# Moving the layer norm, the last group's context parts and the route scatters to other steps of an attention and expert kernel

## The reference

```
s = attention(xn)            # 16 heads of 32, causal, a bias per head that grows with distance
g = silu(ffn(xn))            # router picks one of 2 experts per token:
                             #   h = xn @ w_fc[e].T ; a = where(h >= 0, h, h / 2) ** 2
                             #   out = (a @ w_proj[e].T) * probability of the chosen expert
x = x + s * g
```

## Time and profile before

| | |
|---|---|
| median of 3 runs | 1466.62 us |
| the profiled execution | 1466.41 us |
| its span in the trace | 1464.6 us |
| TensorE busy | 1367.3 us, 93% |
| VectorE, ScalarE, GpSimd busy | 930.0, 773.3, 692.3 us |
| iteration -1 (to the first transposed head) | 66.86 us |
| batches 0 to 7, in order | 81.1, 85.5, 85.6, 85.5, 87.2, 85.5, 85.5, 80.7 us |
| last projections and the experts' part | 721.0 us |

### The profile page before, as it was taken

How to read it: one execution, slowest core, us unless ns; L and a number is a source line. 1 busy time by engine, 2 the same in 40 slices (tenths; PEclk the granted TensorE clock), 3 DMA queues, 4 the chain that set the end, 5 groups by cost and what they waited for, 6 DMA issues and landing times.

```text
span 1464.6 us, 30064 instructions
## 1 busy us (share of the span) xinstructions
PE 1367.3 (93%) x9755; PEld 868.8 (59%) x9755; DVE 930.0 (64%) x2441; ACT 773.3 (53%) x1824; POOL 692.3 (47%) x896
## 2 busy tenths in 40 slices
PE   2879999999999999999779999999999999999995
PEld 1455555655556565555546666666666666666663
DVE  7577777777767777777759955554445555544443
ACT  3478778787878778777846522222222222223221
POOL 0356657465665747566624443433343433333332
PEclk9999999999999999999999999999999999999998
DMA  4435334343533434335347422211111122111100
GB/s 162 145 87 148 125 114 128 107 140 109 148 120 121 126 102 139 112 119 146 103 142 232 148 56 58 53 38 43 55 55 53 50 58 58 43 38 51 46 30 30
DMA packets 119458, 140.56 MB, mean 96 GB/s; under 512 B 48655, under 2 KB 97807, under 8 KB 117136
## 3 DMA queue, kind: packets, MB, share of 16 engines
q1 hardware_dynamic: 110368, 112.81, 25.6%
q0 software_dynamic: 8944, 25.83, 5.7%
HBM read 97.81 MB, written 33.95 MB: 90 GB/s over the span
## 4 chain that ended last, share of the span: by engine, by line
PE 78%; DVE 8%; POOL 6%; ACT 3%; issue 2%; DMA 1%; SPq 0%; DVEq 0%; POOLq 0%; ACTq 0%
PE psF L1142 22%; PE psY L1162 22%; PE psA L353 18%; PE psT L447 7%; PE psA L462 5%; POOL pr L942 4%; PE psS L426 3%; POOL route L970 1%; PE psA L410 1%; DVE pr L858 1%; DVE stat L750 1%; DVE am L637 1%; DVE xT L764 1%; DVE wf L1269 1%; POOL rstd L957 1%
## 5 line engine op out<-in xcount | busy, mean ns | idle before, releaser
L1142 PE MATMUL psF<-xT,wf 128*128 128x256 f16 (+1 forms) x3264 | 368.0, 269 | 0.0
L1162 PE MATMUL psY<-wf,aT 128*128 x1584 | 363.9, 379 | 0.5 <-DVE aT L1322 0.4
L1142 PEld LDWEIGHTS psF<-xT,wf 128*128 x3264 | 312.0, 98 | 63.5
L942 POOL TENSOR_SCALAR pr<-pr,rden 128x128 f32<-128x128 f32 (+3 forms) x512 | 269.9, 546 | 139.9 <-DVE rden L869 138.4
L1396 POOL TENSOR_TENSOR a<-a 128x512 f32<-128x512 f32 (+1 forms) x136 | 156.0, 1147 | 370.4 <-DVE a L1313 369.9
L580 ACT ACTIVATE pr<-pr,mn 128x128 f32<-128x128 f32 (+3 forms) x512 | 282.1, 554 | 0.0
L858 DVE CUSTOM_DVE_ANT_0 pr<-psS,base,nsl 128x128 f32<-128x128 f32 (+3 forms) x512 | 249.7, 543 | 4.0 <-PE psS L426 4.0
L1162 PEld LDWEIGHTS psY<-wf,aT 128*128 128x128 f16 x1584 | 154.5, 98 | 159.0 <-issue 1.4
L447 PE MATMUL psT<-conf,pr 128*128 128x128 f32 x1280 | 205.6, 279 | 18.5 <-POOL pr L942 16.7
L447 PEld LDWEIGHTS psT<-conf,pr 128*128 128x128 f32 x1280 | 156.9, 142 | 81.8 <-POOL pr L942 27.9
L353 PE MATMUL psA<-xT,wqkv 128*128 128x512 f16 x768 | 188.4, 385 | 14.8 <-DVE wqkv L668 13.1
(11 more groups left out here) (157 smaller groups left out, 1352.3 us busy)
## 6 DMA issues: line engine op xcount, KB each, us to landing
qk_parts<-pre SPq DMA_DIRECT2D x64, 256.0 KB, 2.7
qs<-qk_parts SPq DMA_DIRECT2D x128, 128.0 KB, 2.7
ks<-qk_parts SPq DMA_DIRECT2D x128, 128.0 KB, 2.7
wst<-in_wf SPq DMA_DIRECT2D x16, 1024.0 KB
wstage<-in_wf SPq DMA_DIRECT2D x32, 512.0 KB, 4.8
xin<-in_x SPq DMA_DIRECT2D x32, 256.0 KB, 4.5
attn_out<-so SPq DMA_DIRECT2D x32, 256.0 KB, 2.0
xT<-wstage SPq DMA_TRANSPOSE x216, 2.4
```

Source lines behind the costliest of these rows:

```text
L942: nc.gpsimd.tensor_scalar(p_, p_, rden[:, c:c + 1], 32768.0, ALU.mult, ALU.mult).then_inc(s["norm_done"], 1)
L1142: last = nc.tensor.matmul(psF[c % 2][:, k * TT:k * TT + tn], w(e, 2 * hc, hl, kc * 512 + col, P), xT[:, r % 2, x, kc, 0:tn], start=(m == 0 ...
L1162: last = nc.tensor.matmul(psY[r % 2][h][:], aT[:, c % 4, x, k, h * P:(h + 1) * P], w(e, 2 * hc + 1, hl, q * 512, 512), start=(c == 0 and k ...
```

## The change

VectorE: statistics move ahead of the step's casts, within steps 0 and 1. The cast of the last group's context moves from step 2 to step 1, between `masked` and the statistics. Rows are made in steps 3 to 6. GpSimd: the deviations move from step 1 to step 2, ahead of the step's low part. The low part of the last group's context moves from step 2 to step 1, ahead of the low part of k. The scatters of a batch are issued in the next iteration, one in each of steps 4 to 7 (for the last batch two in each of steps 4 and 5).

```diff
+            def context_high(pb, pg):
+                if within(pb, 0, B):
+                    wait(dve, s["ctx_staged"], pb * NG + pg + 1)
+                    wait(dve, s["O_done"], pb * QB + 1)
+                    nc.vector.tensor_copy(cx[:, pg, 0, :], cf[:]).then_inc(s["ctx_hi"], 1)
+
@@ att_vector, iteration
                 masked(3)
+                if step == 1:
+                    context_high(b - 1, NG - 1)
+                if more and step < 2:
+                    ln_stats(2 * step)
+                    ln_stats(2 * step + 1)
                 for args in jobs(b, odd, step, ("q", "k", "x", "o", "logits", "rank")):
                     read_out(*args)
                 turned(2)
-                if more:
-                    if step < 2:
-                        ln_stats(2 * step)
-                        ln_stats(2 * step + 1)
-                    elif step < 6:
-                        ln_apply(step - 2)
+                if more and 3 <= step < 7:
+                    ln_apply(step - 3)
...
-                if j == (3 if g else 2):
-
-                    pb, pg = (b, g - 1) if g else (b - 1, NG - 1)
-                    if within(pb, 0, B):
-                        wait(dve, s["ctx_staged"], pb * NG + pg + 1)
-                        wait(dve, s["O_done"], pb * QB + 1)
-                        nc.vector.tensor_copy(cx[:, pg, 0, :], cf[:]).then_inc(s["ctx_hi"], 1)
+                if g and j == 3:
+                    context_high(b, g - 1)
@@ att_gpsimd
+        def context_low(pb, pg):
+            if within(pb, 0, B):
+                wait(pool, s["ctx_hi"], pb * NG + pg + 1)
+                nc.gpsimd.tensor_tensor(cx[:, pg, 1, :], cf[:], cx[:, pg, 0, :], ALU.subtract
+                                        ).then_inc(s["ctx_lo"], 1)
+
@@ att_gpsimd, iteration (after the norms)
-                for kind, bj, i, _, _ in jobs(b, odd, step, ("q", "k")):
-...
-                if more and step == 1:
+                if more and step == 2:
 ...
-                pb, pg = (b, g - 1) if g else (b - 1, NG - 1)
-                if j == (3 if g else 2) and within(pb, 0, B):
-...
+                if step == 1:
+                    context_low(b - 1, NG - 1)
+                for kind, bj, i, _, _ in jobs(b, odd, step, ("q", "k")):
+...
+                if g and j == 3:
+                    context_low(b, g - 1)
                 if b == B - 1 and step in (10, 12):
                     ffn["gather_x"](pool, 0, 0, (step // 2 - 5,))
-                if more and step in (14, 15):
-
-                    wait(pool, s["meta_ready"], nxt + 1, s["apart_pool"])
-                    for i in (2 * step - 28, 2 * step - 27):
+                if within(b, 0, B) and 4 <= step < (6 if b == B - 1 else 8):
+                    pool.wait_ge(s["meta_ready"], b + 1)
+                    for i in ((2 * step - 8, 2 * step - 7) if b == B - 1 else (step - 4,)):
                         nc.gpsimd.indirect_dma_start(
```

More of the change, by code:

```diff
@@ L958, in iteration @@
                                             ).then_inc(s["rstd_ready"], 1)
-                pb, pg = (b, g - 1) if g else (b - 1, NG - 1)
-                if j == (3 if g else 2) and within(pb, 0, B):
-                    wait(pool, s["ctx_hi"], pb * NG + pg + 1, s["apart_pool"])
-                    nc.gpsimd.tensor_tensor(cx[:, pg, 1, :], cf[:], cx[:, pg, 0, :], ALU.subtract
-                                            ).then_inc(s["ctx_lo"], 1)
+                if step == 1:
+                    context_low(b - 1, NG - 1)
+                for kind, bj, i, _, _ in jobs(b, odd, step, ("q", "k")):
+                    w = int(kind == "k")
+                    wait(pool, s["qk_hi"], (bj * NG + i) * 2 + 1 + w, s["apart_pool"])
+                    nc.gpsimd.tensor_tensor(pre[:, w, 1, :], stage[:, w, :], pre[:, w, 0, :],
+                                            ALU.subtract).then_inc(s["qk_lo"], 1)
+                if g and j == 3:
+                    context_low(b, g - 1)
                 if b == B - 1 and step in (10, 12):
                     ffn["gather_x"](pool, 0, 0, (step // 2 - 5,))
-                if more and step in (14, 15):
-                    wait(pool, s["meta_ready"], nxt + 1, s["apart_pool"])
-                    for i in (2 * step - 28, 2 * step - 27):
+                if within(b, 0, B) and 4 <= step < (6 if b == B - 1 else 8):
+                    pool.wait_ge(s["meta_ready"], b + 1)
+                    for i in ((2 * step - 8, 2 * step - 7) if b == B - 1 else (step - 4,)):
                         nc.gpsimd.indirect_dma_start(
```

## The result

The changed kernel takes 1442.28 us, the median of four runs (1440.97 to 1443.58); the kernel before takes 1467.02 us beside it on the same chip (four runs, 1462.87 to 1468.66). The ratio is 0.9836, with a 95% interval of 0.9813 to 0.9858. The prediction was 1447.5 in a range of 1442 to 1456: right in sign and in mechanism, with the time only 0.3 above the low end. The profiled execution took 1442.62 us with a span of 1440.8, so the span is 23.8 us shorter, where the sum said 18.9.

A forecast was written before the change was run, and what follows sets the result against it. TensorE was taken as the bound, its transposes waiting 16.7 us for GpSimd's norms. Terms 15.2 + 2.0 + 1.4 + 2.1 - 1.2 - 1.1 + 0.5 = 18.9 us gave 1447.5, range 1442 to 1456.

The forecast's parts named there:

- the sum: Whole execution: gains and losses of all terms add to 18.9 us, from 1466.4 to 1447.5.
- Statistics, deviations, context: Steps 0 to 3: earlier norms of head 3 (2.06 us) remove step 3's 2.68 us wait; 2.54 gained per full batch.
- 0.14, as predicted: Step 4 of a full batch: TensorE still waits 0.14 us for the norms of head 4.
- The turn of the batch: Between batches: the 0.21 us wait goes, with its restart worth 0.3 us, seven times, 2.1 us.
- Block 2's row: Step 6, batches 1 to 6: the row comes too late for its transposes, costing 0.2 us six times, 1.2 us.
- The wait predicted at 0.74: Start of step 6: TensorE waits 0.74 us for block 2's row; 0.40 left by idle time, 0.13 by starts.
- Batch 0: Gains 2.0 us, from its 1.77 wait and a short wait of the scores; pays nothing for block 2's row.
- Iterations -1 and 8: Iteration -1: last block copy and weight scales later, -1.1 us; iteration 8: context's cast leaves earlier, +0.5 us.
- The clock: Batch 4, after step 3's wait: the granted clock may no longer fall, up to 1.6 us more gain.
- The queue does not stay late: Rival, GpSimd's steps 1 to 3: norms still take 2.72 us, 0.65 less gain in seven batches, 1452 to 1456; 17%.
- the wait does not move a step on: Rival: all of the 2.5 us comes back before step 4, about 1464.5, no change; 7%.
- Scatters do not get in front of norms: Rival, steps 6 and 7, spare 2.6 and 2.2 us: scatters of 5 us each would give 1482, slower; 4%.

The follow-up runs named there:

- 2: Kernel before, with only the statistics moved ahead of the casts of steps 0 and 1: 1458.12 us, periods of 84.84.
- 3: Changed kernel, with both parts of the last group's context put back at the end of step 2: 1454.81 us, periods of 84.03.
- 4: Changed kernel, with deviations back in step 1 behind the low part of k and rows back in steps 2 to 5: 1450.45 us.
- 10: Changed kernel, with the deviations' instruction given twice: 1450.9 us, periods of 83.87.
- 11: Changed kernel, with the deviations' instruction given three times: 1461.84 us, periods of 85.20.
- experiment 1: Kernel before, with only the scatters moved to steps 4 to 7: 1466.03 us, periods of 85.06.
- experiment 5: Changed kernel, with step 6's projection put ahead of block 2's transposes: 1445.55 us, periods of 82.57.
- experiment 8: Changed kernel, with projection first in step 6, first weight reduction in step 4 instead of 5, iteration -1's rows in steps 2 to 5: 1436.83 us.
- experiment 6: Changed kernel, with rows made in steps 2 to 5 again in iteration -1 alone: 1442.06 us.
- Experiment 12: Kernel before, unchanged, profiled again: 1464.99 us.
- experiment 7: Changed kernel, with every scatter issued three times, the copies into tensors of their own: 1464.99 us, periods of 84.22.
- 9: Kernel of experiment 8, with the deviations moved from step 2 to step 3 behind the norms of head 4: 1438.55 us.

## Why the prediction was right, and where its sizes were off

**Statistics, deviations, context: right.** Step 3's wait is gone, and by starts it was worth 2.67 us, 2.68 in the sum. At step 4 0.19 is lost, with 0.05 given back a step on: 0.14, as predicted. The norms of head 3 take the forecast 2.06. Experiments 2 to 4 show that the statistics alone do not do it and that it fails without either of the other two moves, 10 and 11 that step 4 stands on its edge.

**The turn of the batch was mis-sized**: "0.3" where it is 0.46, the trace's 4.65 against 4.25 us and 0.06 of a quicker restart behind it; experiment 1 alone has 0.48. The step that failed adds 0.1 to the idle time of 0.21. The recorded idle time is about 0.2 short of how late a start is: at step 4 of the changed kernel none is shown and 0.25 is lost (4.48 against 4.23), and the turn of before had 0.21 recorded and 0.43 lost (4.65 against 4.22). In experiments 3, 4, 10 and 11 idle times of 1.47, 1.33, 1.33 and 2.65 go with steps longer by 1.63, 1.49, 1.49 and 2.81, 0.16 more each time. This is 0.16 of the 0.24 missed per batch.

**Block 2's row was mis-sized**: "0.2" where it is 0.10 (step 6 0.16 longer, the next 0.06 shorter; 0.08 in experiment 5). The working gave 0.40 by idle time and 0.13 by starts; starts were right. The wait predicted at 0.74, which was a reading by starts, is 0.73 by starts: block 2's transposes come 1.60 us after the first of their step, 0.87 before. Its idle time is 0.57. The old wait, 0.34 in idle time and 0.60 by starts in the working, was worth 0.68 in the period (experiment 8).

**Batch 0** gained 2.9 and not 2.3. By starts step 2 is 2.09 shorter and step 3 0.31 longer, 1.8 where the working took the idle time of 1.77; steps 0 and 1, whose scores had stood for VectorE, give 0.67, of which the working had some 0.2; the turn gives 0.39. It also has new waits at block transposes (up to 1.70 us), where the prediction had said that it pays nothing; steps 4 to 8 together are as long as before all the same (0.06 shorter).

**Iterations -1 and 8: right.** Last copy of the first rows 11.79 us after the first row, 10.67 before: 1.12 against 1.1, confirmed by experiment 6. In iteration 8 the last wait for the context's low part went from 7.35 to 6.74 us, 0.6 against 0.5. PE's timeline of the kernel before, then of the changed one:

```profile
743.56 12.64 PE L353 MATMUL psA<-wout,cx 128*128 128x512 f16 x48 [7.35 <-POOL cx L962]
```

```profile
719.26 13.48 PE L353 MATMUL psA<-wout,cx 128*128 128x512 f16 x48 [6.74 <-POOL cx L931]
```

**The clock** was in the bounds, and of the 4.9 us beyond the sum it is some 2: 1.7 in batch 4 and 1.7 ahead of batch 0, less about 0.9 in batch 7 and 0.5 in the experts' part. Experiment 12 says that such stretches differ between executions, so the first term is none of the change's. The second is no more so: seven of the fourteen traces have a stretch at the lower clock that starts between 53 and 57 us, the kernel before and experiment 6 among them, and the changed kernel's has not. So the sum came nearer than 23.8 makes it look, and that the time is at the low end of the range is in part luck.

TensorE is also busy for 5.7 us less for the same instructions. Most of that is not the clock: a batch without a stretch at the lower clock has 82.25 us of busy time before and 81.43 after, which makes 4.9 in six. With each wait that is gone a little of what the profile counts as busy is gone too, which fits idle times that understate a wait. Batch 4's clock is 1.6 of the rest, and batch 7 gives 1.8 back.

**The rivals.** The queue does not stay late, and the wait does not move a step on. Scatters do not get in front of norms: 1.31 us is the longest, and spare times of 2.7 us (read as 2.6) and of some 2.2 hold. The Trainium skill (SBUF — State Buffer, A bandwidth-pool intuition that's wrong) would have had 3100 ns beside VectorE's copies; none of the 32 scatters here, 13 of them beside a copy (L851), nor of the 96 of experiment 7, 22 of them beside a row (L763), comes near that: 1.31 us at most in either. The port rule of the Trainium skill (SBUF — State Buffer, Who interferes with whom) is borne out: the cast of q fell from 1.17 to 0.43 when the norms beside it left, and the rows of 1.27 and 1.39 each stand beside a low part of GpSimd.

## What to carry to other kernels

An in-order queue that serves the bound engine should have the work that engine needs next at its head: here the deviations were right one step later and wrong two steps later, since there they made VectorE late. Size a wait by the starts of the waiting engine's steps with and without it, not by its recorded idle time, which here understated one by half (0.34 for 0.68), while another of 0.57 cost 0.10 net, because it stood in front of that one. After a wait is removed, look at which smaller wait it had covered; the next 0.76 us a batch lay in a swap of two jobs and one number of a table.

## What the runs showed of the hardware that was not expected

The stretches at the lower clock. Batch 4 of the kernel before, in windows of 2 us behind its wait at step 3:

```profile
422.00:424.00 2.00, 1.52 (x8) 0.91 (x9) 1.89 (x9) 0.83 (x3) 2.00 (x3) 0.90 0.36 95
424.00:426.00 2.00, 2.00 (x8) 1.31 (x7) 0.00 (x0) 0.66 (x5) 2.00 (x4) 0.50 0.37 131
426.00:428.00 2.00, 2.00 (x10) 0.95 (x9) 0.00 (x0) 1.29 (x4) 0.70 (x2) 0.74 0.00 0
```

A granted clock of 0.50 is the lower of the two levels, 1.2 of 2.4 GHz. In batches 1 to 6 such a fall costs 1.5 to 1.7 us and stands at the end of a wait: here it comes about a microsecond after TensorE started again, and in 1 and 11 the first transposes behind the wait run at the lower clock already (1.12 us against 0.66). It occurred there three times, once each in the kernel before, in 1 and in 11. Their batches, and those of 12, which has none, have a wait of 1.8 to 2.65 us: three in 24. In the other ten traces, the changed kernel and 2 to 10, with waits of at most 1.5 us, none of 60 batches has it. That fits a fall that now and then follows the longer waits, but three cases don't show it, 11's wait of 2.65 set it off only once in six, and in batch 7 a fall stands behind shorter waits too (1.11 us at 670 us in 3, 1.42 at 690 us in the changed kernel). It stays open.

A scatter held GpSimd for 0.95 to 1.31 us in every trace, beside rows and copies of VectorE too, and one right behind another starts 0.30 us after its end, where it is 0.15 to 0.20 behind other instructions. The deviations' power takes GpSimd 1.04 us for 4 numbers per row, nearly as much as the low part of 512 (1.16), and the addition and multiplication just ahead of it, on the same 4 numbers, 0.20 (L956 in the timeline of POOL above).
